# Causal attention: query projections split over two steps, query transposes one step later

## The reference

```
h = _rmsnorm(hidden_states, ln1_w)
q = (h @ Wq).reshape(B, S, NH, HD)      # NH = 32, HD = 128
k = (h @ Wk).reshape(B, S, KVH, HD)     # KVH = 4
v = (h @ Wv).reshape(B, S, KVH, HD)
q = _rope(q, pos)
k = _rope(k, pos)
k = jnp.repeat(k, rep, axis=2)          # rep = 8
v = jnp.repeat(v, rep, axis=2)
scores = einsum('bqhd,bkhd->bhqk', q, k) / sqrt(HD), causal mask
attn = jax.nn.softmax(scores, axis=-1)
o = einsum('bhqk,bkhd->bqhd', attn, v).reshape(B, S, NH * HD) @ Wo
x = resid + o
```

## Time and profile before

| what | value |
| --- | --- |
| three runs | 1317.99, 1318.99, 1319.39 us; median 1318.99 |
| the profiled execution: span, first to last instruction | 1316.0 us |
| its own time (no separate one was recorded; the median stands for it) | 1318.99 us, 3.0 more than the span |
| PE busy with matmuls | 1118.8 us (85%) |
| PE busy with weight loads | 903.7 us (69%) |
| DVE, ACT, POOL busy | 918.5, 615.4, 628.4 us (70, 47, 48%) |
| mean granted TensorE clock | 0.921 |

### The profile page before, as it was taken

How to read it: one execution, slowest core, us unless ns; L and a number is a source line. 1 busy time by engine, 2 the same in 40 slices (tenths; PEclk the granted TensorE clock), 3 DMA queues, 4 the chain that set the end, 5 groups by cost and what they waited for, 6 DMA issues and landing times. The chain is left out here.

```text
span 1316.0 us, 22382 instructions
## 1 busy us (share of the span) xinstructions
PE 1118.8 (85%) x6634; PEld 903.7 (69%) x6636; DVE 918.5 (70%) x2116; ACT 615.4 (47%) x1837; POOL 628.4 (48%) x653
## 2 busy tenths in 40 slices
PE   5499988796377665699989998999997999999998
PEld 4366655585122222588988888888887888888887
DVE  4676684733799997587777777888787555555555
ACT  4266633321544442266656655666555333333332
POOL 3633260454255554256546644664443455555554
PEclk9699979687688886799999999999998899999999
DMA  7000000003000000200200010000001111111111
GB/s 222 1 1 0 0 0 10 1 0 106 0 0 0 0 0 10 72 2 1 73 4 1 12 62 4 1 1 1 2 1 26 37 48 43 42 47 48 48 48 44
DMA packets 41706, 33.63 MB, mean 26 GB/s; under 512 B 5872, under 2 KB 39696, under 8 KB 41520
## 3 DMA queue, kind: packets, MB, share of 16 engines
q1 hardware_dynamic: 39888, 31.35, 8.0%
q10 hardware_dynamic: 1728, 1.18, 0.3%
HBM read 31.47 MB, written 1.05 MB: 25 GB/s over the span
## 5 line engine op out<-in xcount | busy, mean ns | idle before, releaser
L1756 POOL TENSOR_TENSOR hid_l<-hid,hid_h 128x512 fp32r<-128x512 f32 x66 | 85.6, 1297 | 131.4 <-ACT hid_h L1725 131.4
L1381 POOL TENSOR_TENSOR qr<-r_part_a,r_part_b 128x512 f32<-128x512 f32 x64 | 82.4, 1288 | 127.4 <-DVE r_part_b L1415 126.2
L1395 POOL TENSOR_TENSOR prob<-prob,rden 128x128 f32<-128x128 f32 (+1 forms) x256 | 124.5, 510 | 37.9 <-DVE rden L1466 37.9
L1806 DVE TENSOR_TENSOR hid<-psum,silu 128x512 f32<-128x512 f32 x66 | 45.7, 692 | 129.6 <-ACT silu L1723 129.6
L1341 ACT ACTIVATE prob<-psum,neg_max 128x128 f32<-128x128 f32 (+1 forms) x256 | 106.0, 424 | 38.3 <-DVE neg_max L1455 33.3
L902 POOL TENSOR_TENSOR drive<-u,b_all 128x1024 f32<-128x1024 f32 x32 | 78.0, 2441 | 86.0 <-DVE h L1014 56.5
L1014 DVE TENSOR_TENSOR_SCAN h<-decay,drive 128x1024 f32<-128x1024 f32 x32 | 107.2, 3353 | 8.6 <-POOL drive L902 5.8
L1798 DVE SCALAR_TENSOR_TENSOR x<-psum,weight,x 128x256 f32<-128x256 f32 x264 | 108.9, 475 | 0.0
L73 PE MATMUL psum<-xt_h,gu_l 128*128 128x512 f32 x264 | 105.7, 400 | 2.4 <-POOL gu_l L1741 2.4
L75 PE MATMUL psum<-xt_h,gu_h 128*128 128x512 f32 x264 | 104.5, 396 | 0.0
L74 PE MATMUL psum<-xt_l,gu_h 128*128 128x512 f32 x264 | 104.2, 395 | 0.0
(11 more groups left out here) (260 smaller groups left out, 3801.2 us busy)
## 6 DMA issues: line engine op xcount, KB each, us to landing
early<-in_L_ffn_Wq_dram SPq DMA_DIRECT2D x4, 1024.0 KB, 5.7
early<-in_L_ffn_Wo_dram SPq DMA_DIRECT2D x4, 1024.0 KB, 8.5
raw<-in_L_ffn_Wg_dram SPq DMA_DIRECT2D x32, 128.0 KB, 2.2
raw<-in_L_ffn_Wu_dram SPq DMA_DIRECT2D x32, 128.0 KB, 2.3
raw<-in_L_ffn_Wd_dram SPq DMA_DIRECT2D x32, 128.0 KB, 2.2
x<-_attn_hidden_states_dram SPq DMA_DIRECT2D x8, 128.0 KB, 4.6
early<-in_L_ffn_w_up_q_dram SPq DMA_DIRECT2D x1, 1024.0 KB, 5.9
early<-in_L_ffn_w_up_scale_dram SPq DMA_DIRECT2D x4, 256.0 KB, 7.4
```

Source lines behind the costliest of these rows:

```text
L1381: pool.tensor_tensor(qr[:, i, :], part_a[:, slot, :], part_b[:, slot, :], ALU.add).then_inc(roped, 1)
L1395: ins = pool.tensor_tensor(at, at, rden[:, s % 2, i:i + 1].to_broadcast([P, (i + 1) * P]), ALU.mult)
L1756: pool.tensor_tensor(hid_l[:, j, cols], hid[:, c, :], f(hid_h[:, j, cols]), ALU.subtract)\
```

## The change

The query projection on PE is cut in two entries of the schedule, `q_begin` (the wait for the bank and the product of k half 0) and `q_end` (the product of k half 1, and the signal). They stand in successive steps: for m even, i = 0 begins in r=2 and ends in r=3, i = 1 begins in r=3 and ends in r=4; for m odd, i = 0 begins in r=5 and ends in r=6, i = 1 begins in r=7 and ends in r=0 of the batch row that uses it. DVE's rotation and POOL's sum follow `q_end`. Query transposes move one step later, from r=5, 6 to r=6, 7 and from r=1, 2 to r=2, 3. In `FIRST` the last projection is only begun.

```
--- before.py
+++ after.py
@@ -1254,27 +1254,34 @@
                     yield "peak", *at(1)
                 if n >= 1 and (not last or n < STEPS + 1):
                     yield "turn_probs", *at(-1)
-                if own and r in (1, 2):
-                    yield "turn_q", gg, 2 * b + 1, r - 1
+                if own and r in (2, 3):
+                    yield "turn_q", gg, 2 * b + 1, r - 2
                 if more and r == 4:
                     yield "turn_k", *ahead_b(gg, b + 1)
-                if more and r in (5, 6):
-                    yield "turn_q", *ahead(gg, 2 * b + 2), r - 5
+                if more and r in (6, 7):
+                    yield "turn_q", *ahead(gg, 2 * b + 2), r - 6
                 if n >= 2 and (not last or n < STEPS + 2):
                     yield "values", *at(-2)
                 if n >= 3:
                     yield "project_out", *at(-3)
                 if more and r == 1:
                     yield "kv", *ahead_b(gg, b + 1)
+                if own and r == 0:
+                    yield "q_end", gg, 2 * b + 1, 1
                 if more and r in (2, 3):
-                    yield "q", *ahead(gg, 2 * b + 2), r - 2
-                if more and r in (6, 7):
-                    yield "q", *ahead(gg, 2 * b + 3), r - 6
+                    yield "q_begin", *ahead(gg, 2 * b + 2), r - 2
+                if more and r in (3, 4):
+                    yield "q_end", *ahead(gg, 2 * b + 2), r - 3
+                if more and r in (5, 7):
+                    yield "q_begin", *ahead(gg, 2 * b + 3), (r - 5) // 2
+                if more and r == 6:
+                    yield "q_end", *ahead(gg, 2 * b + 3), 0
                 if not last and 6 <= s < 6 + 2 * PIECES and s % 2 == 0:
                     yield "weights", gg + 1, (s - 6) // 2
 
-        FIRST = [("kv", 0, 0), ("q", 0, 0, 0), ("q", 0, 0, 1), ("turn_k", 0, 0), ("turn_q", 0, 0, 0),
-                 ("turn_q", 0, 0, 1), ("q", 0, 1, 0), ("q", 0, 1, 1), ("scores", 0, 0), ("peak", 0, 0)]
+        FIRST = [("kv", 0, 0), ("q_begin", 0, 0, 0), ("q_end", 0, 0, 0), ("q_begin", 0, 0, 1), ("q_end", 0, 0, 1),
+                 ("turn_k", 0, 0), ("turn_q", 0, 0, 0), ("turn_q", 0, 0, 1), ("q_begin", 0, 1, 0), ("q_end", 0, 1, 0),
+                 ("q_begin", 0, 1, 1), ("scores", 0, 0), ("peak", 0, 0)]
 
         def run(eng, does):
 
@@ -1395,7 +1402,7 @@
                         ins = pool.tensor_tensor(at, at, rden[:, s % 2, i:i + 1].to_broadcast([P, (i + 1) * P]), ALU.mult)
                     ins.then_inc(p_normed, 1)
 
-                run(pool, dict(q=q, kv=kv, softmax=softmax, weights=weights))
+                run(pool, dict(q_end=q, kv=kv, softmax=softmax, weights=weights))
 
             @block.vector
             def _(dve):
@@ -1480,7 +1487,7 @@
                     dve.tensor_tensor(at, psum[:, WOB, :].rearrange("p (t n) -> p t n", t=2), at, ALU.add)\
                         .then_inc(z_added, 1)
 
-                run(dve, dict(q=q, kv=kv, turn_q=turn_q, turn_k=turn_k, peak=peak, turn_probs=turn_probs,
+                run(dve, dict(q_end=q, kv=kv, turn_q=turn_q, turn_k=turn_k, peak=peak, turn_probs=turn_probs,
                               softmax=softmax, values=values, project_out=project_out))
 
             @block.tensor
@@ -1493,20 +1500,23 @@
                 pe.sem_inc(p_lo, 1)
                 pe.sem_inc(o_lo, 1)
 
-                def q(g, m, i):
+                def q_half(g, m, i, k):
+                    b = m // 2
+                    where = ds((g & 1) * KD + k, 1)
+                    cols = slice((m % 2) * QC, (m % 2 + 1) * QC)
+                    return product(pe, psum[:, PROJB[i], :], core.xt(k, slice(b * S + i * P, b * S + (i + 1) * P)),
+                                   (wq_h[:, where, cols], wq_l[:, where, cols]), k == 0, k == KD - 1)
+
+                def q_begin(g, m, i):
                     before = bank_user_before(q_index(g, m, i), m, i)
-                    bank = psum[:, PROJB[i], :]
                     if not known(before, 0):
                         pe.wait_ge(parts, before + 1)
                     if m == 0 and i == 0:
                         pe.wait_ge(w_ready, 2 * g + 1)
-                    b = m // 2
-                    for k in range(KD):
-                        where = ds((g & 1) * KD + k, 1)
-                        cols = slice((m % 2) * QC, (m % 2 + 1) * QC)
-                        ins = product(pe, bank, core.xt(k, slice(b * S + i * P, b * S + (i + 1) * P)),
-                                      (wq_h[:, where, cols], wq_l[:, where, cols]), k == 0, k == KD - 1)
-                    ins.then_inc(projected, 1)
+                    q_half(g, m, i, 0)
+
+                def q_end(g, m, i):
+                    q_half(g, m, i, 1).then_inc(projected, 1)
 
                 def bank_user_before(index, m, i):
 
@@ -1593,7 +1603,7 @@
                     if h == REP1 - 1:
                         ins.then_inc(wo_done, 1)
 
-                run(pe, dict(q=q, kv=kv, turn_q=turn_q, turn_k=turn_k, scores=scores, turn_probs=turn_probs,
+                run(pe, dict(q_begin=q_begin, q_end=q_end, kv=kv, turn_q=turn_q, turn_k=turn_k, scores=scores, turn_probs=turn_probs,
                              values=values, project_out=project_out))
```

## The result

The changed kernel takes 1325.32 us (median; 1324.17 to 1325.73), the kernel before 1319.19 beside it (1317.99 to 1319.44): a ratio of **1.0046, 95% interval 1.0034 to 1.0059**. It is slower by 6 us; forecast were 3. The profiled execution took 1325.07 us, its span is 1323.1.

The account below looks back on a forecast made before the run. PE was taken as the bound, with holes waiting for POOL's division. New holes of 37.6 us against 34.3 gave +3.3, the start -0.2: +3.1 on 1319.0 made 1322.1 us, range 1318.3 to 1326.

Parts of the forecast that it names:

- The rule of a hole: PE waits unless the step after a projection's end lasts 3.34 us, or 4.58 with a weight piece behind POOL's sum.
- r5 and r6 together: PE's hole over steps 5 and 6 modulo 8: 0.68 us without a weight piece, 1.92 with one.
- r0 behind a piece: PE's hole at step 0 modulo 8, after a weight piece two steps earlier: 1.29 us.
- The base case: Attention stage: new holes 37.6 us against 34.3, total 1322.1; the range 1320 to 1325 got chance 0.55.
- PE's gap of 1.69 stays: Ends of the loop's body: both such steps stay 1.69 us longer than their work, 3.4 together.
- The scores' wait at r=3: Score products wait for DVE's subtraction of the later query transposes: 0.2 us (0 to 0.3) without another hole.
- r0 without a piece: Step 0 modulo 8, following a projection's end and a step of 3.34 us: no hole.
- The start: First steps of attention: 1.3 us earlier at step 3, with 1.14 of work moved behind it: -0.2.
- Rival A: Weight pieces on POOL cost nothing new and evened steps decide: -22 us, 1297; chance 0.10.
- B: POOL's sum of step 6 waits for step 7's query transposes, 0.42 us in 15 rows: +6.3, 1328; chance 0.10.
- C: Separated k halves lower PE's clock: 8 us if a tenth of 64 projections lose 1.2, 1330; chance 0.03.
- D: Nothing changes: score waits and small hole extras are 0, the start gives 1 us: -0.4, 1318.6; chance 0.22.

Follow-up runs that it names:

- experiment 1: Changed kernel with its nine weight pieces per head moved to steps where no query sum stands ahead of them on POOL: 1302.42 us, 0.9878 of the kernel before.
- experiment 2: Kernel before with its weight pieces moved to steps without a query sum on POOL: 1316.93 us, 0.9995 of the unedited kernel before.
- experiment 5: Changed kernel with all nine weight pieces of a head behind query sums, in place of seven: 1332.72 us, 1.0106 of the kernel before.
- experiment 4: Kernel before with only the query transposes one step later, projections whole and in place: 1318.92 us, 1.0005 of the kernel before.
- experiment 3: Changed kernel with the split undone, whole projections where their second halves stood: 1359.35 us, 1.0298 of the kernel before.
- experiment 6: Changed kernel with the loop's body cut after r=3 in place of r=2: 1329.27 us, 1.0078 of the kernel before.
- experiment 8: Changed kernel, pieces off the sums, second even projection's first half in r=4, loop cut after r=4: 1298.71 us, 0.9844 of the kernel before.
- experiment 7: Changed kernel, pieces off the sums, first half of the second even projection moved from r=3 to r=4: 1299.88 us, 0.9861 of the kernel before.

## Why the prediction came out as it did

**The rule of a hole** held everywhere. Measured and, in brackets, forecast: r5 and r6 together 0.65 to 0.69 without a piece (0.68) and 1.87 to 1.91 with one (1.92); r0 behind a piece 1.32 to 1.34 (1.29); r2 behind one 0.99 to 1.03 (1.00); r1, r4 and r7 nothing (0). In the last head a batch row takes 27.6 (27.5), a middle row of the first three 30.8 (30.8). Experiments 1, 2 and 5 show that the pieces' place decides, 4 that the later transposes alone cost nothing, 3 that the split saves time against whole projections at the later places. The base case had the mechanism and the sign right: with q_end at r4 and r0 seven of nine pieces stand behind a sum where before it were five, with a shorter step behind them.

**The size was off: 3.1 forecast, 6 measured.** The time of 1325.3 lies within the stated range, but 0.3 above what the base case alone was given. The forecast is a small difference of two large sums of holes, and the terms below missed by 2.8, nearly as much as the difference itself. They all missed the same way; as large an error the other way would have made it no change at all, so that the sign came out had some luck in it. All holes and loop ends beyond the work are 43.8 in place of 37.6 + 3.4 = 41.0 for steps 3 to 124. The terms of the sum that were mis-sized:

- "PE's gap of 1.69 stays" was wrong. The two loop ends take 2.28 and 2.41 beyond the work, +1.3 in all. The step that holds them keeps its length (5.62 and 5.75, before 5.72): less work stands in the same time. With the body cut behind a whole projection it is 0.9 to 1.1 (experiments 6 and 8). That products in PE's queue cover a part of the loop's end would fit this, but not all of the record: the kernel before has a whole projection in front too and takes 1.7, and in experiment 3, where no projection stands in front, it is 2.0 and 2.1, less than behind half a one. What sets the gap stays open.
- The scores' wait at r=3, taken as 0.2, is 0.21 to 0.23 in the last head (0.12 seen at r2, 0.10 behind it), but 0.40 once in each of the first three heads: there the subtraction starts 3.09 into the step and not 3.00, and PE follows it later still. The trace of the kernel before has the same 3.10 in the fourth batch row of each of these heads, so it could have been read there; why is open. +0.6.
- r0 without a piece, taken as nothing, is 0.03 to 0.09, six times; behind a piece 0.04 more than forecast, nine times. +0.8.
- The start: 1.20 earlier at step 3 with 1.14 of work moved, -0.06 in place of -0.2.

**Rival A** (1297) gave the size of what the new order can do, but for a kernel whose pieces are elsewhere: experiment 1, at 1302, is that kernel. **B** fell: POOL's sum stands 1.65 into r7 in all fifteen rows, 0.02 later than before. **C** did not act in the profiled execution of the changed kernel: its clock is 1.00 through both loop ends. 61 of the 64 projections are split, and all ran at 1.00 but the first half of the first one, which stands in the slow clock that both kernels have at the start of the stage; in the kernels of the experiments the clock fell behind long idle stretches only. So the trace does not bear out what the prediction drew from the Trainium skill (TensorE: Matmul & The Clock Gate, on why this matters for kernels), that the split would cost clock; that row of the page speaks of k tiles with transfers between them, and here other matmuls stand between. The same section's advice to leave no long idle stretches between bursts is borne out in kind, but not in size: the clock fell here behind shorter ones than those it warns of (below), and the measurement decides. **D** fell by the same terms that made the sum larger: it put the scores' wait at 0 and the gain at the start at 1 us, where 0.2 to 0.4 and 0.06 were measured.

## What to carry to other kernels

Where an engine works through its queue in order, a filler instruction costs next to nothing or its whole length (here 1.24 us), by what stands behind it: place it behind the instruction that the bound engine waits for, not ahead. When an order of work is evened out, the fillers have to be placed anew with it; neither edit alone was a gain here, both together 1.2%, with the two further moves of experiments 7 and 8 1.6%. Forecast such a schedule by one rule with few constants per step, and check which steps the end of a loop falls on.

## What the runs showed of the hardware that was not expected

Behind an idle stretch of PE inside the dense stage the clock can fall to 1.2 GHz for a part of the next step, 1.6 us lost each time. In the ten profiles all idle stretches up to 1.79 us (36 of them of 1.4 or more) were followed by a granted clock of 1.00; of 18 between 1.85 and 2.66 us, 13 were followed by 0.57 to 0.65 over the next 4 us. Three more, of 2.31 and 2.32 us in the first steps of the stage, were followed by 1.00. So the length of the stretch alone does not decide it. The changed kernel's loop ends (2.13 and 2.26) are among the 18 and kept their clock in the profiled run; whether they do in every execution was not seen.
